# A hybrid convolution, attention and expert kernel: the first stage's VectorE, ScalarE and TensorE work taken in another order, five taps moved around the mixing, strips copied in mixed order

## What is computed

```python
x = x + conv_ref(group_norm(x), w2, p6w, w7, w8, p9w)
# conv_ref on the normalised image:
t1  = seven copies of x, shifted by 2k - 6 columns
t2  = conv 1x3 over x
t3  = einsum('nakhw,nbhw->nakb', t1, x)      # sums of products: the Gram matrices
t9  = p9w * p6w * t3                         # the weights of the mixing
t10 = einsum('nakb,nakhw->nbhw', t9, t4)     # t4: seven copies of t2, shifted by k - 3 rows
t7  = depthwise conv 1x5 over t2
t8  = depthwise conv 5x5, dilation 2, over x
out = t8 - t10 + t7
# then, over 3136 tokens of 32 channels per image:
t = t + attention(layer_norm(t)) + layer_norm(t)
t = t + experts(layer_norm(t))               # eight experts, the best two of each token
```

## Time and profile before

| | |
|---|---|
| median of 3 runs | 2905.97 us (2905.68 to 2910.04) |
| the profiled execution's own time | 2911.31 us |
| its span in the trace | 2909.5 us |
| TensorE busy, over the span | 2476.8 us (85%) |
| VectorE busy | 2394.3 us (82%) |
| ScalarE busy | 1660.7 us (57%) |
| the four passes of the first stage | 23.1 to 590.5 us |
| the pass without new images | 590.5 to 656 us |

### The profile page before, as it was taken

The page is one execution under the profiler, slowest core; times in us unless marked ns, Lnnn a source line. Parts: engine busy times, 40 slices in busy tenths (PEclk is TensorE's granted clock), DMA queues, the critical chain, the costliest instruction groups (busy, mean ns, idle before and its releaser), DMA issues. The chain is left out here.

```text
span 2909.5 us, 48420 instructions
## 1 busy us (share of the span) xinstructions
PE 2476.8 (85%) x18630; PEld 1005.7 (35%) x18630; DVE 2394.3 (82%) x4268; ACT 1660.7 (57%) x2202; POOL 321.5 (11%) x401
## 2 busy tenths in 40 slices
PE   3858586744999999999999999999999997787786
PEld 1332323221222222222222222222222227676664
DVE  4466566567999999999999999999999945888787
ACT  1152524251777777777777777777777772333323
POOL 0000000010000000000000000000000002554545
PEclk9988888855999999999999999999999995666666
DMA  7885949233010112111011011011010001222210
GB/s 166 187 220 152 246 128 246 95 130 112 1 57 1 57 57 73 46 57 47 11 57 57 1 57 57 1 57 57 2 57 23 23 7 73 96 73 72 95 67 23
DMA packets 61563, 220.99 MB, mean 76 GB/s; under 512 B 15910, under 2 KB 28834, under 8 KB 54690
## 3 DMA queue, kind: packets, MB, share of 16 engines
q1 hardware_dynamic: 60146, 214.41, 25.1%
q10 hardware_dynamic: 1200, 3.69, 0.3%
HBM read 81.67 MB, written 74.60 MB: 54 GB/s over the span
## 5 line engine op out<-in xcount | busy, mean ns | idle before, releaser
L1196 DVE TENSOR_REDUCE at_XM<-at_psX 128x1 f32<-128x448 f32 x2688 | 1546.0, 620 | 88.2 <-PE at_psX L1059 67.6
L1125 ACT ACTIVATE at_PR<-at_psS 128x896 f32<-128x896 f32 x1344 | 1163.1, 915 | 448.3 <-PE at_psS L1039 446.2
L1077 PE MATMUL at_psV<-at_PR,at_V 128*32 128x448 f32 x5376 | 645.3, 552 | 0.1
L1039 PE MATMUL at_psS<-at_US,at_KS 128*128 128x448 f16 x2688 | 635.8, 356 | 0.6 <-ACT at_PR L1125 0.2
L1059 PE MATMUL at_psX<-at_KS,at_US 64*128 64x448 f16 x1344 | 489.7, 364 | 62.0 <-DVE at_XM L1196 42.9
L1059 PE MATMUL at_psX<-at_KS,at_UH 64*128 64x448 f16 x1344 | 489.8, 364 | 0.0
L1059 PEld LDWEIGHTS at_psX<-at_KS,at_US 64*128 64x128 f16 x1344 | 124.5, 93 | 716.7 <-DVE at_XM L1196 660.3
L1039 PEld LDWEIGHTS at_psS<-at_US,at_KS 128*128 128x128 f16 x2688 | 201.0, 98 | 273.5 <-ACT at_PR L1125 117.5
L1463 POOL TENSOR_TENSOR fi_WE<-fi_WE 128x256 f32<-128x256 f32 (+1 forms) x224 | 213.1, 979 | 172.8 <-DVE fi_WE L1517 171.7
L1174 POOL CAST at_mrow<-at_mt 7x128 f16<-7x128 f32 x64 | 18.0, 281 | 1652.5 <-DVE at_mt L1215 1652.5
L393 PE MATMUL psA<-sb_stacks,sb_lhs 128*32 128x448 f32 x1568 | 171.4, 566 | 15.2 <-DVE sb_X L766 7.7
(11 more groups left out here) (188 smaller groups left out, 2123.8 us busy)
## 6 DMA issues: line engine op xcount, KB each, us to landing
sums<-at_O SPq DMA_DIRECT2D x16, 1568.0 KB, 6.3
fi_SUMS<-sums SPq DMA_DIRECT2D x16, 1568.0 KB, 6.7
sb_stacks<-sb_T SPq DMA_DIRECT2D x64, 270.5 KB, 5.8
sb_stacks<-sb_Xp SPq DMA_DIRECT2D x64, 248.8 KB, 5.1
sb_stacks<-sb_Xp SPq DMA_DIRECT2D x64, 248.0 KB, 4.9
at_KS<-key_stacks SPq DMA_DIRECT2D x16, 784.0 KB, 7.8
at_US<-query_stacks SPq DMA_DIRECT2D x16, 784.0 KB, 10.6
sb_stacks<-sb_T SPq DMA_DIRECT2D x64, 172.5 KB, 3.8
```

The costliest lines, as they stand in the source:

```text
L1039: last = nc.tensor.matmul(psS[:, at % 2, k, 0:TILE], KS[:, b, (2 * c + k) * P:(2 * c + k + 1) * P], US[:, b, t * TILE:(t + 1) * TILE], sta ...
L1077: last = nc.tensor.matmul(psV[C * q:C * q + C, 0:TILE], V[:, b, G * k + q, :], PR[:, (n * 2 * STEPS + 2 * q4 + q // 2) % PRS, q % 2, :], s ...
L1125: nc.scalar.activation(PR[:, f % PRS], psS[:, at % 2, :, 0:TILE], ACT.Exp).then_inc(p_ready, 1)
L1196: nc.vector.tensor_reduce(o, psX[:, (at + j) % 3, 0:TILE], AX.X, ALU.max).then_inc(x_done, 1)
```

## The change

Four things change, all in `prepare`.

1. **Strips.** Both fills take the 16 strips in a fixed mixed order in which successive strips read from the lower and the upper 64 partitions in turn; the half written alternates in most places too.
2. **SyncE.** The load of the next group's x stands ahead of the stores of token tile 2, and `store_tokens` of tile 3 behind the first half of the next group's strips.
3. **TensorE.** `turn_keys` of token tiles 0 and 1 moves from behind `correlate` of image 1 to behind that of image 2. The queries of token tile 0 go between the conv3 tiles of half 1 (two after each), and those of token tile 1 go between taps of conv5 tiles 0 and 1. Taps 0 and 1 of conv5 tile 0 stand ahead of the two summing matmuls, taps 2 to 4 of tile 0 and taps 0 to 4 of tile 1 behind them and ahead of the wait for `lhs10`; then taps 5 and 6 of both. Token tile 2 stands beside conv5 tiles 2 and 3, token tile 3 beside tiles 5 and 6.
4. **VectorE and ScalarE.** `token_norm` is cut into `centre`, `scale` and `low_parts`, `mixing` into `mixing` and `new_weights`, and the pieces stand in another order. The mixing now comes ahead of token tile 2, whose normalisation stands between the adds; token tile 3's stands behind the next group's normalisation. ScalarE copies image 0 of half 1 ahead of the squares of token tile 1.

The diff, cut to its core:

```diff
+        HG = G // 2
+        STRIP_ORDER = [p for k in range(G) for j in range(HG) for p in ((j, (HG + j + k) % G), (HG + j, (j + k) % G))]
...
@@ SyncE, fill_stacks and fill_stacks2
-                for n in range(G):
-                    for s in range(G):
-                        sp.dma_start(XS[C * s:C * s + C, n, a:z],
+                for n, s in STRIP_ORDER:
+                    sp.dma_start(XS[C * s:C * s + C, n, a:z],
...
@@ SyncE, step
                 if old:
-                    store(m, 1)
-                    store_tokens(m, 2)
+                    store_tokens(m, 1)
+                    store_stacks(m, 1)
                 if more:
                     sp.wait_ge(taps_done, g + 1)
...
                     load(g + 1)
                 if old:
+                    store_tokens(m, 2)
                     store_stacks(m, 2)
-                    store_tokens(m, 3)
                 if more:
                     sp.wait_ge(xp_ready, g + 2)
                     sp.wait_ge(conv5_full, g * NT + 4)
                     fill_stacks(g + 1, 0)
                 if old:
+                    store_tokens(m, 3)
                     store_stacks(m, 3)
...
@@ TensorE, step
                 for h in range(2):
-                    keys, queries_in = keys_of(h), queries_of(h)
                     for i in ((0, 1, 2), (3, 4, 5, 6))[h]:
                         conv3(g, i)
+                        run(ask(2))
                     turn_stack(g, 0, h)
                     turn_stack(g, 1, h)
                     correlate(g, 0, h)
                     turn_stack(g, 2, h)
                     correlate(g, 1, h)
-                    run(keys)
                     turn_stack(g, 3, h)
                     correlate(g, 2, h)
-                    run(queries_in[0:4])
+                    run(keys_of(h))
                     correlate(g, 3, h)
-                    run(queries_in[4:7])
-                if new:
-                    for i in range(2):
-                        pe.wait_ge(gram_out, g * 2 + i + 1)
-                        nc.tensor.matmul(psT[:, i], adder[:], (gsb, gT)[i][:], ...)
-                    pe.wait_ge(lhs10_ready, g + 1)
-                    between = {0: keys_of(2), 1: queries_of(2), 4: keys_of(3), 5: queries_of(3)}
-                    for i in range(NT):
-                        conv5(g, i, between.get(i, ()))
-                    turn_output(g)
+                    asked[:] = queries_of(h)
+
+                pe.wait_ge(t2_ready, g * NT + NT)
+                conv5(g, 0, range(0, 2), ask(2))
+                mix(g)
+                conv5(g, 0, range(2, 5), ask(3))
+                conv5(g, 1, range(0, 5), ask(2))
+                pe.wait_ge(lhs10_ready, g + 1)
+                for i in range(2):
+                    conv5(g, i, range(5, 7))
+                between = {2: keys_of(2), 3: queries_of(2), 5: keys_of(3), 6: queries_of(3)}
+                for i in range(2, NT):
+                    conv5(g, i, beside=between.get(i, ()))
+                turn_output(g)
...
@@ ScalarE, step
                 for h in range(2):
+                    if h == 1 and old:
+                        keys(m, 0)
                     for i in ((0, 1, 2), (3, 4, 5, 6))[h]:
                         to_t2(g, i)
+                        if h == 1 and old:
+                            query_high(m, 0, range(NT)[2 * (i - 3):2 * (i - 2)])
...
+                    if h == 1 and old:
+                        squares(m, 1)
+                    turned(g, 1, h, slice(0, 2))
+                    if h == 1 and old:
+                        deviations(m, 1)
+                    turned(g, 1, h, slice(2, None))
+                    if h == 0 and old:
+                        high_parts(m, 0)
                     turned(g, 2, h)
-                    if old:
-                        high_parts(m, h)
-                        keys(m, h)
+                    if h == 1 and old:
+                        high_parts(m, 1)
                     turned(g, 3, h)
-                    if old:
-                        query_high(m, h)
+                if old:
+                    keys(m, 1)
+                    query_high(m, 1)
...
@@ VectorE, step
+                    centre(m, 0)
+                    taps5((1,))
+                    scale(m, 0)
+                    taps5((2,))
+                    low_parts(m, 0)
+                    taps5((3,))
                     query_low(m, 0)
+                    centre(m, 1)
+                    taps5((4,))
+                    scale(m, 1)
+                    low_parts(m, 1)
+                else:
+                    taps5((1, 2, 3, 4))
+                dve.wait_ge(t2_ready, g * NT + NT)
+                taps_row((0, 1))
+                mixing(g)
+                if old:
+                    query_low(m, 1, tiles=range(0, 3))
+                new_weights(g)
+                if old:
+                    query_low(m, 1, tiles=range(3, NT))
+                taps_row((2, 3, 4))
+                dve.wait_ge(taps_done, g + 1)
+                add((0,))
+                if old:
+                    centre(m, 2)
+                add((1,))
+                if old:
+                    scale(m, 2)
+                    low_parts(m, 2)
+                add((2,))
+                if more:
+                    statistics(g + 1)
                 if old:
                     query_low(m, 2)
+                add((3,))
+                if more:
+                    normalise(g + 1)
+                if old:
+                    centre(m, 3)
+                add((4,))
+                if old:
+                    scale(m, 3)
+                    low_parts(m, 3)
+                add((5,))
                 if old:
                     query_low(m, 3)
+                add((6,))
```

More of the change, by code:

```diff
@@ L274, in fill_stacks2 @@
                 sp.wait_ge(t2_ready, g * NT + (3 if h == 0 else NT))
[L275 to L278, removed]
+                for n, s in STRIP_ORDER:
+                    sp.dma_start(T2S[C * s:C * s + C, n, a:z],
+                                 T2[C * n:C * n + C, YW * s + a:YW * s + z]).then_inc(t2s_in[h], 16)
             def store(m, n, z=first, alone=False):
@@ L378, in correlate, with conv5 @@
                         last.then_inc(gram_done, 1)
-            def conv5(g, i, beside=()):
+            def conv5(g, i, taps=range(7), beside=()):
                 if i >= 2:
                     pe.wait_ge(x1_ready, g * NT + i - 1)
-                for j in range(7):
+                for j in taps:
                     if j == 5 and i in (0, 2):
@@ L395, in conv5, with mix @@
                         last.then_inc(conv5_full, 1)
-                    if j < len(beside):
-                        part, *args = beside[j]
+                    if j - taps[0] < len(beside):
+                        part, *args = beside[j - taps[0]]
                         part(*args)
+            def mix(g):
+                for i in range(2):
+                    pe.wait_ge(gram_out, g * 2 + i + 1)
+                    nc.tensor.matmul(psT[:, i], adder[:], (gsb, gT)[i][:], start=True, stop=True).then_inc(gram_sum, 1)
             def turn_output(g):
@@ L494, in turned @@
                     act.wait_ge(gram_done, g * 2 * G + h * G + n - 1)
-                for k in HALVES[h]:
+                for k in HALVES[h][part]:
                     u = turned_set(n, h, k)
@@ L574, in step @@
                     query_high(m, 2)
-                    squares(m, 3)
-                    deviations(m, 3)
-                    high_parts(m, 3)
                 if more:
@@ L581, in step @@
                 if old:
+                    squares(m, 3)
+                    deviations(m, 3)
+                    high_parts(m, 3)
                     keys(m, 3)
-                if old:
                     query_high(m, 3)
@@ L713, in token_norm, with low_parts @@
                 nc.vector.tensor_tensor(z.XH, z.XH, per_token(lrs), ALU.mult).then_inc(xh_ready, 1)
+            def low_parts(m, n, z=first):
+                r = m * G + n
                 dve.wait_ge(xh_ready, r + 1)
@@ L722, in token_norm, with query_low @@
                 nc.vector.memset(z.XH[:, :, 0:1], 1.0).then_inc(val_ready, 1)
-            def query_low(m, n, z=first):
-                for i in range(NT):
+            def query_low(m, n, z=first, tiles=range(NT)):
+                for i in tiles:
                     dve.wait_ge(u_hi, (m * G + n) * NT + i + 1)
```

62 lines of the change are left out of this document (20 added, 42 removed).

## The result

| | time, us | against before |
|---|---|---|
| before, beside it | 2907.74 median (2905.68 to 2910.04, 4 runs) | |
| after | 2891.65 median (2890.36 to 2892.84, 4 runs) | 0.9944 [0.9927, 0.9962] |
| profiled execution after | 2892.84, span 2891.0 | before 2911.31, span 2909.5 |

The kernel became 16 us faster, 0.56%. The forecast was 2872 (34 us faster): the sign was right and the time lies in the range, but the move is less than half of what the sum gave. The pass lengths show where. A pass goes from the start S of one `SCALAR_TENSOR_TENSOR` over all of `sb_X` to the next (in the last one to the first reduction of the pass behind); c is the start of the centring of token tile 1.

What follows compares the result with a forecast made beforehand. No engine is full; a pass is a chain of waits, with strip DMAs setting c. Gains of 3.6, 7.5, 9.8 and 13.0 us in passes 0 to 3 total 33.9: 2872 us by the median, range 2860 to 2899.

Steps and rivals of the forecast that it cites:

- One sign of being wrong: Passes 1 to 3: c early but more than 112 us behind it would put the error into the late part's chain.
- I take 20%, between the two: Strip fills: the mixed order cuts strip time by 20%, between 12% and 31%; `XS` half 1 and `T2S` half 0 give 6.7 us.
- Its mechanism: Strip DMAs: the higher rate was tied to the source half changing, which the mixed order does at every strip.
- 6% less: Strip fills: the skill's 6% for two partition halves, strips at 0.94 of their time; some -15 us, 2891; strips little or no faster 0.28.
- The late part loses 3.3 us a pass: From c to the pass end: 109.3 us where it was 106.0, through two token norms TensorE waits for; 1.9 in pass 3.
- 1 us per pass: Conv5 after the longer waits: TensorE restarts at its lower clock level, charged 1 us per pass.
- Lands before the statistics at c + 54; if late, add 2 waits: Early load of the next group's x: waits for `taps_done` at c + 42, lands before c + 54; costed at nothing.
- Pass 0, forecast 3.6 us shorter: Pass 0: 16 strips before its first conv3 give 4.1 us, less 0.5 for two taps ahead of the sum.
- the floor of S + 32.7: Start of token tile 1's centring: the chain from `t2_zero` to low queries 0 allows c no earlier than S + 32.7.
- Strips no faster: Rival on the strip fills: the order leaves strip time unchanged, total -6.6 us, 2899; strips little or no faster 0.28.
- The token norms in the open decide: Rival on the late part: c not at least 3.3 us earlier, so +9 us, 2915; slower or unchanged 0.10.
- Faster still: Rival on a shorter late part: 31% less strip time and no restart cost, -41 us, 2865; chance 0.12.

Runs made afterwards that it cites:

- the kernel with the old order: The kernel after with the strips back in the nested order (n outer, s inner), all else as changed: 2906.67 us, 0.9989.
- the source alternating: The kernel before with only the strip order changed, s outer and n as 0, 2, 1, 3, so the source half changes every strip: 2910.11 us, 1.0003.
- the strips alone: The kernel before with the strips in the mixed order and nothing else changed: 2886.76 us, 0.9918.
- the fillers: The kernel after plus matmuls whose result nothing reads, in three TensorE waits of each pass: 2882.58 us, 0.9905.
- the early part alone: The kernel after up to token tile 1's norm, with the late order of the kernel before on all four engines: 2883.27 us, 0.9905.
- the statistics early: The kernel after with the next group's statistics ahead of add 2 in passes 1 and 2: 2887.78 us, 0.9918; with unread filling matmuls too, 2876.58 us, 0.9880.

## Why the prediction was off

Of the 17.7 us of pass time that are missing (33.9 forecast, 16.2 measured), 13.6 belong to the strip term and 4.1 to the schedule, by the kernel with the old order. Two of the prediction's signs of being right came true, the waits of about 10 us for `y16_ready` and no 14 us wait at the mixing. One sign of being wrong came true as well: in pass 2, c is early and 112.2 us lie behind it.

- **The step that failed: "I take 20%, between the two", the strips' time.** A strip's rate rose from 204 to 236 and 225 GB/s, so its time fell by 14% and 9%, and by 9% in the two windows without the 325. The bound of 31% came from charging to one strip all that a window of 3 us gained, in which nearly three strips moved. Read as rates, the 222 and 236 GB/s of the earlier trace rows give 8% and 14% less time, and that is what came. From the first strip to the next token load, pass 1 went from 58.9 us (116.83 to 175.70, old order) to 51.8 (116.82 to 168.62), pass 2 from 40.4 to 36.0: 12% and 11%. Against the old order c came 7.2, 4.4 and 4.4 us earlier in passes 1 to 3 and pass 0 got 0.2 us shorter, where 10.8, 6.2, 6.2 and 4.1 were forecast; 2.5 us of it were lost again behind c. SyncE's issue time fell by more than the transfers' time, and what the issues saved, the store behind them partly gave back, 8.7 us to the load instead of 4.5. The prediction took a duration on the issuing queue for the transfer's.
- **Its mechanism was wrong as well.** Not the source half alone but source and destination together: 204 and 201 GB/s with the source alternating.
- **"6% less" was no better.** The Trainium skill ("SBUF — State Buffer", section "Can I just issue two DMAs to hit both halves?") would make the rate, as an estimate from its 6%, some 216 GB/s and gave 2891, the measured time. But the windows show 223 to 236, 10% and more, and the strips alone gave 2886.8: the time agrees by luck, since the late part lost more than forecast, and the rate does not.
- **"The late part loses 3.3 us a pass" was too small.** It lost 4.2, 6.3 and 2.4. Up to the keys of token 2 the chain held: mixing at c + 21.8 (21.7), add 0 from c + 42.3 to c + 42.9 (42.3 to 43.0), `y16_ready` at c + 53.6 (53.8). Then tile 2's rest took 9.5 us for 7.6, tile 3 9.6 for 8.3, tile 5 9.3 for 7.6. Of tile 3's 9.6 us, 1.36 are the wait for a drained query bank; in tiles 2 and 5 it is the clock. I had put "1 us per pass" for it; the fillers, which take away the restarts, shorten the part by 2.4 to 3.5 us. The clock was in the earlier trace rows, as a first tap of 1.72 us for 0.77, and I charged it too little: behind the wait of 8.89 us all taps up to 376.9 take 1.72 us, those from 377.62 on 0.96, and the 10 us behind the wait have a mean granted clock of 0.74.
- **"Lands before the statistics at c + 54; if late, add 2 waits" pointed at the wrong side.** The data was there. The order put the statistics behind add 2, which waits for TensorE, and the fourth query then waited for VectorE, 1.36 us in each of two passes. Moving them took the wait away and shortened the way between the two key sets by 2.1 and 1.2 us, of which pass 1 kept 0.1.
- **Pass 0, forecast 3.6 us shorter, became 2.1 longer.** With the old strip order it is 2.3 longer. The two taps stand ahead of the sum, while the three row taps of 10.5 us set the time to add 0 in both; TensorE then stands 3.85 us before conv5 tile 2 instead of 0.43 and restarts at the lower clock. The kernel before has there:

```profile
100.41 26.70 PE L393 MATMUL psA<-sb_stacks,sb_lhs 128*32 128x448 f32 x280 [0.43 <-DVE sb_X L766]
```

  The same five tiles take 28.3 us in the kernel after, 1.6 more, and start 0.5 later, which is the 0.5 that I had costed for the taps. I had no restart in the sum, and the 4.1 us of the strips were lost at the second conv3 block.
- **c.** In pass 2 the floor of S + 32.7 was right as VectorE's own (its last low query of token 0 ended at S + 32.9), but the load came at S + 30.9 and landed at S + 34.6: the DMAs still set c, by 1.7 us.
- **The rivals.** "Strips no faster" is what the old order shows, at 2906.7 instead of 2899: its gain was 3.8 us and not 6.6. "The token norms in the open decide" did not come true as a whole, since c came 7.8 us or more earlier, but it had the right place: beside the early part alone, the late order costs the 11.3 us that the experiment shows. "Faster still" fell with both of its conditions.

What stays open is why strips that change both halves are faster, why an alternating source alone shortens SyncE's issues, and why pass 0's second conv3 block loses its clock in some kernels and keeps it in others (the granted clock between 60 and 65 us is 0.82 in the kernel after, but no experiment was aimed at it). A cover for the wait in which the next group's normalisation also stays early wasn't tried.

## What to carry to other kernels

A wait removed from TensorE's queue is only gained when no new one stands behind it: lay out every engine's queue from the moved instruction on, and charge every long hole with the slow clock for as long behind it as a trace shows it, here 5 us behind 9 us of waiting. When a change has two independent parts, ask what each gives alone; here a few lines of DMA order gave more than the whole. Size a transfer by when the next thing that depends on it lands, not by how long its issues take.

## What the hardware showed that was not expected

- Strips of 254 KB, 32 partitions to 32 partitions, moved at 203 to 210 GB/s in the nested order and at 200 to 211 with only the source or only the destination half alternating (leaving out a first microsecond's burst), and at 223 to 235 when nearly every strip changed both: 0.9918 of the kernel's time for an order.
- SyncE issued 32 such strips in 37.1 us in the nested order and in 21.9 us with the source half alternating, at 203 and 204 GB/s.
- TensorE work that computes nothing paid: the granted clock stayed at 1.00 (2.4 GHz) through stretches where it had been 0.50 to 0.74 after idling, and the kernel became 11 us faster (0.9944 to 0.9905 by the ratios, and with the statistics early 0.9918 to 0.9880).
